# Gated delta rule on one core: the chunk inverse in seven products instead of eight, gate exponentials placed earlier, output halves dealt out in pairs

## The reference, cut to what matters

```python
g = cumsum(g)
decay = where(tril, exp(g[..., :, None] - g[..., None, :]), 0.0)
M = where(stril, einsum('bhncd,bhnmd->bhncm', k_beta, k) * decay, 0.0)
T = solve_triangular(eye + M, eye, lower=True)
v_c, k_cumdecay = T @ v_beta, T @ (k_beta * exp(g))
# scan over chunks: v_new = v_i - kcd_i @ state; out_i = q_i e^g @ state + attn @ v_new
# then RMS norm, times silu(z), times W_out
```

## Time and profile before

| what | value |
|---|---|
| time, median of 3 runs | 3435.7 us (3433.08 to 3445.15) |
| profiled execution | 3442.66 us, span 3440.2 us |
| mean granted TensorE clock | 0.985 |
| busy: TensorE, its weight loads, VectorE, ScalarE, GpSimd | 93%, 74%, 73%, 58%, 46% |

### The profile page before, as it was taken

The page is one execution under the profiler, slowest core; times in us unless marked ns, Lnnn a source line. Parts: engine busy times, 40 slices in busy tenths (PEclk is TensorE's granted clock), DMA queues, the critical chain, the costliest instruction groups (busy, mean ns, idle before and its releaser), DMA issues. The chain is left out here.

```text
span 3440.2 us, 57288 instructions
## 1 busy us (share of the span) xinstructions
PE 3198.9 (93%) x18210; PEld 2536.0 (74%) x18210; DVE 2510.4 (73%) x5351; ACT 1980.4 (58%) x4826; POOL 1584.7 (46%) x2825
## 2 busy tenths in 40 slices
PE   0249999999999999999999999999999999999977
PEld 0238787787877878778877878778787788878753
DVE  7756777777777777777777777777777777777743
ACT  6725665566555665556655666555655566555631
POOL 7643545444454445444454545444454535454310
PEclk9989999999999999999999999999999999999978
DMA  3322222222222322222222222222222222232102
GB/s 112 127 60 74 83 82 59 83 84 74 70 78 82 87 78 61 83 85 71 82 65 83 87 77 75 72 82 75 77 65 83 86 77 88 59 83 80 41 7 110
DMA packets 295389, 265.67 MB, mean 77 GB/s; under 512 B 221584, under 2 KB 250384, under 8 KB 285840
## 3 DMA queue, kind: packets, MB, share of 16 engines
q1 hardware_dynamic: 286160, 131.99, 15.6%
q10 hardware_dynamic: 8928, 130.03, 10.2%
HBM read 232.30 MB, written 29.62 MB: 76 GB/s over the span
## 5 line engine op out<-in xcount | busy, mean ns | idle before, releaser
L689 PE MATMUL x<-xs,w_high 128*128 128x512 f32 x3072 | 1054.3, 424 | 24.0 <-POOL w_low L1336 13.5
L922 ACT ACTIVATE uvec<-rb,cpos 128x128 f32<-128x128 f32 x512 | 160.0, 364 | 856.6 <-PE rb L709 856.6
L689 PE MATMUL x<-xs,w_low 128*128 128x512 f32 x1536 | 609.0, 396 | 0.0
L689 PEld LDWEIGHTS x<-xs,w_high 128*128 128x128 f32 x3072 | 525.8, 191 | 87.8 <-POOL w_low L1336 14.0
L998 ACT ACTIVATE slot<-lane 128x512 fp32r<-128x512 f32 x640 | 364.5, 649 | 147.7 <-PE lane L813 147.7
L1319 POOL TENSOR_TENSOR block_step<-block_in 64x14 f32<-64x14 f32 (+6 forms) x896 | 229.6, 256 | 341.6 <-DMA block_in<-blocks_dram 220.3
L689 PEld LDWEIGHTS x<-xs,w_low 128*128 128x128 f32 x1536 | 289.8, 189 | 66.4
L1295 POOL TENSOR_TENSOR lower<-bt,offdiag 128x512 fp32r<-128x512 f32 x128 | 163.3, 1276 | 366.1 <-DVE bt L1171 361.5
L1078 DVE SCALAR_TENSOR_TENSOR cacc<-x,cwv,cacc 128x511 f32<-128x511 f32 (+2 forms) x384 | 281.7, 747 | 38.3 <-ACT cacc L909 3.5
L1078 DVE SCALAR_TENSOR_TENSOR cacc<-x,cwqk,cacc 128x511 f32<-128x511 f32 (+2 forms) x384 | 281.2, 746 | 27.1 <-ACT cacc L909 5.9
L1321 POOL TENSOR_TENSOR block_in<-block_in,block_step 64x14 f32<-64x14 f32 (+6 forms) x896 | 237.3, 265 | 131.1 <-issue 5.9
(11 more groups left out here) (230 smaller groups left out, 7458.4 us busy)
## 6 DMA issues: line engine op xcount, KB each, us to landing
xs<-mix_dram ACTq DMA_DIRECT2D x62, 2048.0 KB, 7.7
gb<-cum_dram SPq DMA_DIRECT2D x128, 256.0 KB, 4.2
w_in<-in_w_qkvz SPq DMA_DIRECT2D x48, 512.0 KB, 4.1
w_out<-in_w_out SPq DMA_DIRECT2D x16, 512.0 KB, 5.8
blocks_dram<-bt SPq DMA_DIRECT2D x512, 8.0 KB, 1.5
inverse_dram<-block_out SPq DMA_DIRECT2D x64, 128.0 KB, 2.2
inv<-inverse_dram SPq DMA_DIRECT2D x512, 16.0 KB, 1.9
xacc<-in_x SPq DMA_DIRECT2D x4, 1024.0 KB, 10.8
```

Of the source, the lines that this page charges most:

```text
L689: ins = mm(PROJ_BANK[kind][i][:, :], w, x, start=(k == 0 and j == 0), stop=(k == KC - 1 and j == 2))
L922: ins = a(uvec[:, h, :], rb[:, sl(h, HD)], ACT.Copy, scale=sm2[p]["cpos"][:, ch, h:h + 1])
```

## The change

The sum of powers is written as P + X2 (P + X2 (P + X2 P)), P standing for P + X P after job 2 here and X2 for the square of X. It has ten jobs in place of eleven, and the pipeline 19 slots in place of 20; `FIRST` stays 9. Evictions that add: jobs 2, 4, 5, 6, 8, 9; copies by ScalarE: 0, 1, 3, 7 (six before).

```
-SLOTS = 20
-JOBS = 11
+SLOTS = 19
+JOBS = 10
-        kks = sq[:, 0, :]...
+        kks = sq[:, 1, :]...
-        ADDED = (4, 6, 7, 9, 10)
+        ADDED = (2, 4, 5, 6, 8, 9)
...
                 (lower, natural),
                 (natural, lower),
+                (s0, turned),
                 (s1, s0),
-                (s0, s1),
-                (s0, turned),
-                (lower, s2),
                 (s2, pinv),
-                (s0, pinv),
+                (s2, s0),
+                (s2, s1),
                 (pinv, None),
                 (None, s1),
                 (s2, pinv),
```

```
                     elif k == 14:
                         out(1, 0)
+                        out(1, 1)
                     elif k == 15:
-                        out(1, 1)
-                    elif k == 16:
                         out(2, 0)
                         out(2, 1)
+                    elif k == 16:
+                        out(3, 0)
                     elif k == 17:
-                        out(3, 0)
-                    elif k == 18:
                         out(3, 1)
```

```
                         elif k == 10:
                             query_squares(l)
+                        elif k == 11:
+                            exp_decay(l, 0)
                         elif k == 12:
-                            exp_decay(l, 0)
-                        elif k == 14:
                             exp_decay(l, 1)
+                        elif k == 13:
                             exp_small(l, p)
```

```
+                dve.drain()
+                v.tensor_tensor(kks, x0[...], t["strict"][...], ALU.mult)
...
-                if h == 0:
-                    W("kk_full", l + 1)
-                    v.tensor_tensor(kks, x0[...], t["strict"][...], ALU.mult)
-                    dve.drain()
...
-                    if job == 4:
+                    if job == 2:
                         ins = v.tensor_tensor(pinv[:, h, :, :], made, turned[:, h, :, :], ALU.add)
-                    elif job in (6, 7):
-                        ins = v.tensor_tensor(pinv[:, h, :, :], made, pinv[:, h, :, :], ALU.add)
-                    elif job == 9:
+                    elif job in (4, 5, 6):
+                        dst = {4: s0, 5: s1, 6: pinv}[job]
+                        ins = v.tensor_tensor(dst[:, h, :, :], made, pinv[:, h, :, :], ALU.add)
+                    elif job == 8:
```

SyncE (`scatter_blocks`) waits for the previous pair's job 2 in place of job 4 before it overwrites the block inverses, and GpSimd (`off_blocks`) for job 1 in place of job 5 before it overwrites `lower`:

```
-                        await_product(sp, m - 1, h, 4)
+                        await_product(sp, m - 1, h, 2)
...
-                        pool.wait_ge(prod_full[h], JOBS * m + 6)
+                        pool.wait_ge(prod_full[h], JOBS * m + 2)
```

More of the change, by code:

```diff
@@ L508, in attention_phase @@
         block_out = sb("block_out", [NB * HPG * NCH, 2, BLK, BLK], F32R)
-        kks = sq[:, 0, :].rearrange("p (c s) -> p c s", s=CH)
+        kks = sq[:, 1, :].rearrange("p (c s) -> p c s", s=CH)
         attn2 = [sb(f"attn{i}", [P, HPG, NCH, CH]) for i in range(2)]
@@ L1048, in _ @@
             s0, s1, s2 = slot
-            DEST = [s0, s1, s2, lower, pinv, s0, pinv, pinv, s1, s2, None]
+            DEST = {0: s0, 1: s1, 3: s2, 7: s1}
             LOOP(act, body)
@@ L1124, in key_sums @@
                 v.tensor_reduce(sums[:, 0, :], work, AX.X, ALU.add)
+                dve.drain()
+                v.tensor_tensor(kks, x0[:, :].rearrange("p (c s) -> p c s", s=CH),
+                                t["strict"][:, :].unsqueeze(1).to_broadcast([P, NCH, CH]), ALU.mult)
             def query_sums(l):
@@ L1162, in b_matrix @@
             def b_matrix(l, h, p):
-                if h == 0:
-                    W("kk_full", l + 1)
-                    v.tensor_tensor(kks, x0[:, :].rearrange("p (c s) -> p c s", s=CH),
-                                    t["strict"][:, :].unsqueeze(1).to_broadcast([P, NCH, CH]), ALU.mult)
-                    dve.drain()
                 W("decay_ready", 2 * l + h + 1)
@@ L1230, in body @@
                         add_out(n, 3)
-                    if A and k - FIRST in ADDED:
+                    if A and k - FIRST in ADDED and k - FIRST > 2:
                         finish_product(m, k - FIRST, 1 - p)
@@ L1244, in body @@
                     if A:
+                        if k - FIRST == 2:
+                            finish_product(m, 2, 1 - p)
                         if k == 1:
@@ L1276, in body @@
                             b_matrix(l, 0, p)
-                        elif k == 15:
+                        elif k == 14:
                             b_matrix(l, 1, p)
-                    if B and k in (15, 16, 17):
-                        add_out(n, {15: 0, 16: 1, 17: 2}[k])
+                    if B and k == 15:
+                        add_out(n, 0)
+                    elif B and k == 16:
+                        add_out(n, 1)
+                        add_out(n, 2)
             LOOP(dve, body)
```

## The result

The changed kernel takes 3599.1 us (median of 4 runs, 3592.0 to 3602.0), the kernel before 3438.3 (4 runs). The ratio is 1.0463, 95% interval 1.0447 to 1.0480. The change is slower by 161 us. I had forecast 3540, 3500 to 3590; the time lies 9 us outside the range and at the place of rival 2 (3595).

A forecast was written before the change was run, and what follows sets the result against it. TensorE was taken to bound the kernel, slot by slot. Per iteration + 2.2 (wait) - 0.89 (removed job) + 0.4 (clock); times 62: + 82 + 25 = + 107 us, less some 3: about 3547 profiled, 3540 median; range 3500 to 3590.

The forecast's parts named there:

- rival 2: TensorE's clock falls at nearly every wait for the SiLU of gate z: + 80 + 80 us, about 3595; chance 0.08.
- What bounds the kernel: Attention stage: TensorE bounds it slot by slot, an output half costs 0.86 us, and every wait adds to the time.
- Rival 3: Attention slots bound by latency: halves cost 0.51 us, TensorE catches up with the wait over seven slots, 3411; chance 0.04.
- The wait for SiLU z: First output half waits for ScalarE's SiLU of gate z behind head 0's exponentials: begins 2.2 us later, bounds 2.0 to 2.4.
- Behind the wait: Slots after the first output half: each again set by TensorE, VectorE margins 0.5 to 1.1 us, no further cost.
- halves in pairs: Output halves dealt two at a time: cost nothing; without that cover, adds behind the B matrices cost about 1 us each.
- block inversion: Gather starts about 0.9 us later; inverted blocks land 3 us ahead of the product that wants them: hidden.
- evictions: ScalarE loses four copies, VectorE gains two adds; with second-mix scans job 3 starts some 0.4 us late, hidden.
- The clock: TensorE's clock falls to 1.2 GHz behind a third of the waits, 0.4 us per iteration, 25 us; bounds 0 to 80.
- Rivals 4: ScalarE: one table set serves both functions, no load added, SiLU z on time, - 55 us, 3380; chance 0.02.
- 5: ScalarE issues the Exp load before the squares, in idle time; SiLU z is 0.9 late: 3436; chance 0.03.
- 6: Each ScalarE table switch costs as much again as its load: + 159 us on top of 80, about 3674; chance 0.02.

The follow-up runs named there:

- the longer iteration: The changed kernel with six more unused matmuls in slot 14, behind the wait, 1.3 us more work per iteration: 3704.7 us, ratio 1.0772.
- the wait of 3.1 us: The kernel before with only the gate exponentials moved up (head 0 to slot 11, head 1 to 12, small ones to 13): 3792.4 us, ratio 1.1024.
- the SiLU first: The changed kernel with the SiLU of gate z put ahead of head 0's exponentials in slot 11, two table loads per iteration: 3588.4 us, ratio 1.0435.

## Why the prediction was right in kind and too small

*What bounds the kernel: right.* A half is 0.86 us, and slots are TensorE's. The removed job gives back 0.77 us per iteration where nothing else is in the way (the version with the B matrices later) and without the exponentials' move the rest of the change is a gain of 1.4%. Rival 3 (slots bound by latency) is out: a wait of 2.2 us was not caught up in the slots behind it.

*The wait for SiLU z: right.* Place and cause are as worked out, and the first half begins 2.2 us later, as forecast. Net it is 1.12 us per iteration in the trace against 1.3. From median to median it is 1.20 (48.07 to 49.27); every fourth iteration of before lasted some 48.35, and that excess is gone in the changed kernel. Undone, it takes 207 us with it (the clock included), and alone in the kernel before it adds 3.1 us per iteration, as worked out from the same rows. The table loads are half of the story: without the one ahead of z the first half begins 1.4 us earlier; but with the loads gone and the exponentials still ahead of a copy, the loss is the same.

*Behind the wait, halves in pairs, block inversion, evictions: right.* The one new wait, job 3's for the adds of job 2, had been foreseen: in a quarter of the iterations job 3 begins 0.4 us later (9.18 us into the iteration against 8.80), some 0.4 forecast, and that is hidden by the larger wait. The pairs are worth 1.4 us per iteration where I had said about 1 for each of the two adds.

*The clock: this step failed.* I wrote "I take a third of the iterations, 0.4 us each, 25 us". It measured 1.4 us per iteration, 88 us: 63 us too little. The whole miss is 59 us (3599 against 3540), because the wait net of the removed job, at 69 us, came 10 below its term (82 less 3). Two sizes in the clock's term were wrong, and the share weighs more: with the share as measured and my price it would have been 63 us, with my share and the price as measured 34.

The share: I said the light spot's place "will wander" and took a third; it was 51 of 60. It walks, but slowly: an iteration of 50.93 us moves it by 0.27 us, so that falls come in rows of six or seven. With iterations 1.4 us longer the share is 73%. Why it is as high as that, and what sets it, stays open.

The price of a fall: I said "products hardly pay" and took 1.2 us; a fall costs 1.66, and a product job with a half takes 3.44 us against 1.78, double. The trace of before had the rows for this, in the stretch at 0.50 of the earlier trace rows:

```profile
276.23 1.97 PE L813 MATMUL lane<-identr,pinv 128*128 128x128 f32 x8 [0.53 <-DVE pinv L1187]
278.03 3.76 PE L813 MATMUL lane<-slot,bt 128*128 128x128 f32 x16
```

One product job takes 1.80 us there from its start to the next one's, against the 0.89 of the earlier trace rows. I did not use them. The upper bound that I gave ("nearly every time", 1.3 us per iteration, 80 us) was too low as well, since 1.4 us and 88 were measured with falls in 85% of the iterations.

Rival 2 had the right mechanism, a fall at nearly every wait; that its 3595 lies 4 us from the measured time is partly luck, because its two terms of 80 us measured 69 and 88. Rivals 4, 5 and 6 are out by the timeline of ScalarE: each load stands right before its function and the function begins 0.01 us behind it.

## What to carry to other kernels

Before moving a step up an in-order queue, list what stands behind it there and which of those the bound engine waits for at once: here 2.5 to 3.8 us of exponentials and table loads went ahead of a SiLU and a copy of 0.6 us each, which TensorE needs at once. Then subtract the idle time that the engine had ahead of them (1.7 us ahead of the SiLU, next to none ahead of the copy). If the bound engine is TensorE, price a new wait twice: its length, and the stretch at 1.2 GHz behind it, in which the product jobs and the halves of this kernel took about double. A cheap test of the second is to fill the wait with unused matmuls: if the program gets faster, it was the clock.

## What was not expected of the hardware

Falls of the clock lasted 3.4 us where they began after the wait had ended and 6.8 us where they began before or within 0.1 us of its end (22 and 22 in the longer iteration, 17 and 42 with the wait of 3.1 us). Two long ones with the SiLU first began 0.5 us behind its wait, as did short ones, so this isn't the whole rule. They cost 1.66 and 3.2 us, about half of their length: at 1.2 GHz a half takes 1.66 us against 0.86 and a product job 1.80 against 0.89. With 1.1 us of unused matmuls in the wait of 2.2 us none of 60 iterations had a fall, and a booked wait of 0.7 us ahead of a product (the halves dealt singly) brought none.
